# x of a Mamba2 layer brought to token order by VectorE's 32x32 blocks and DRAM instead of TensorE

## The reference, cut to what matters

```
gate, xBC, dt = split(xn @ in_proj_w.T)
x, B, C = split(silu(conv4(xBC) + conv_b))
xdt = x * dt                                    # per token and head
scores = (C @ B.T) * Lmat                       # chunk by chunk, Lmat = exp(cs_l - cs_s), lower triangle
Ydiag  = scores @ xdt
states = B.T @ (decay * xdt)                    # one per chunk, then a scan over the chunks
Yoff   = C @ prev_state * exp(cs)
y = (Ydiag + Yoff + x * D) * silu(gate), normed in each group, @ out_proj_w.T
```

## Time and profile before

| | us |
|---|---|
| median of 3 runs | 1758.66 (1757.75 to 1759.58) |
| profiled execution, its own time | 1758.21 |
| its span in the profile | 1756.4 |
| PE busy | 1742.4 |
| DVE busy | 1402.7 |
| ACT busy | 1221.6 |
| POOL busy | 1232.1 |

### The profile page before, as it was taken

One profiled execution on the slowest core, in us unless ns is written; L12 is line 12 of the kernel. 1 busy time (PEld: TensorE's weight loads), 2 busy tenths in 40 slices (PEclk: granted clock), 3 DMA queues, 4 the chain that ended last, 5 costly groups with the idle time before them and its releaser, 6 DMA issues.

```text
span 1756.4 us, 30305 instructions
## 1 busy us (share of the span) xinstructions
PE 1742.4 (99%) x10301; PEld 1459.3 (83%) x10301; DVE 1402.7 (80%) x2211; ACT 1221.6 (70%) x2456; POOL 1232.1 (70%) x877
## 2 busy tenths in 40 slices
PE   8999999999999999999999999999999999999999
PEld 6788888888888888888888888888888888888877
DVE  7978788878878788778788788878887887868941
ACT  6986677777776777777867778767877787643320
POOL 5677777777876787677776777677777787576630
PEclk9999999999999999999999999999999999999999
DMA  5442333333333343333333333333323343236522
GB/s 196 165 131 99 116 116 112 98 123 109 134 105 94 104 135 109 108 101 117 118 102 118 116 111 108 103 109 127 123 91 103 109 135 107 76 98 175 146 78 96
DMA packets 122595, 202.84 MB, mean 115 GB/s; under 512 B 23056, under 2 KB 60560, under 8 KB 122192
## 3 DMA queue, kind: packets, MB, share of 16 engines
q1 hardware_dynamic: 120720, 197.32, 34.8%
q10 hardware_dynamic: 1728, 3.65, 0.5%
HBM read 193.57 MB, written 7.34 MB: 114 GB/s over the span
## 4 chain that ended last, share of the span: by engine, by line
PE 94%; DVE 3%; issue 1%; POOL 1%; DMA 0%; ACT 0%; SPq 0%; DVEq 0%; ACTq 0%; POOLq 0%
PE bank L143 17%; PE bank L145 16%; PE bank L144 16%; PE bank L573 10%; PE bank L609 7%; PE bank L677 7%; PE bank L679 7%; PE bank L678 6%; PE bank L888 3%; PE bank L738 3%; DVE z L1246 1%; PE bank L700 0%; DVE lm L1267 0%; PE bank L720 0%; DVE acc L1337 0%
## 5 line engine op out<-in xcount | busy, mean ns | idle before, releaser
L964 ACT ACTIVATE lm<-lm,hp 128x128 f32<-128x128 f32 x1024 | 313.1, 389 | 0.8
L1246 DVE SCALAR_TENSOR_TENSOR z<-bank,cw_all,z 128x511 f32<-128x511 f32 (+2 forms) x384 | 286.9, 747 | 13.3 <-ACT z L1000 4.2
L1611 POOL TENSOR_TENSOR conv_lo<-raw_x,conv_hi 128x512 fp32r<-128x512 f32 x124 | 203.7, 1643 | 129.4 <-ACT conv_hi L901 129.3
L143 PE MATMUL bank<-xn_hi,conv_hi 128*128 128x512 f32 x640 | 261.4, 408 | 1.9 <-DVE z L1246 1.4
L1306 DVE TENSOR_TENSOR xdt<-bank,hp 128x512 f32<-128x512 f32 x128 | 88.2, 689 | 212.4 <-PE bank L738 212.4
L145 PE MATMUL bank<-xn_hi,conv_lo 128*128 128x512 f32 x640 | 250.6, 392 | 0.0
L144 PE MATMUL bank<-xn_lo,conv_hi 128*128 128x512 f32 x640 | 249.5, 390 | 0.0
L1594 POOL TENSOR_TENSOR yt<-yt,ec 128x384 f32<-128x384 f32 x128 | 146.8, 1147 | 139.3 <-DVE ec L1315 107.9
L1280 DVE SCALAR_TENSOR_TENSOR lm<-lm,gm 128x1024 f32<-128x1024 f32 x128 | 225.3, 1760 | 7.8 <-ACT lm L964 7.2
L1578 POOL TENSOR_TENSOR y_lo<-yt,y_hi 128x512 fp32r<-128x512 f32 x128 | 180.1, 1407 | 52.4 <-ACT y_hi L1035 52.4
L143 PE MATMUL bank<-xn_hi,gate_hi 128*128 128x512 f32 x512 | 212.9, 416 | 0.0
(11 more groups left out here) (152 smaller groups left out, 4051.5 us busy)
## 6 DMA issues: line engine op xcount, KB each, us to landing
lm<-cs_d SPq DMA_DIRECT2D x128, 512.0 KB, 4.5
raw_x<-w_conv_dram SPq DMA_DIRECT2D x128, 256.0 KB, 3.5
ec<-e_d SPq DMA_DIRECT2D x256, 96.0 KB, 2.7
raw_o<-w_out_dram SPq DMA_DIRECT2D x64, 256.0 KB, 3.0
raw_g<-w_gate_dram SPq DMA_DIRECT2D x61, 256.0 KB, 3.2
raw_g<-w_conv_dram SPq DMA_DIRECT2D x16, 256.0 KB, 3.2
raw_o<-w_conv_dram SPq DMA_DIRECT2D x14, 256.0 KB, 3.4
q_raw<-w1q_dram SPq DMA_DIRECT2D x10, 256.0 KB, 3.9
```

The costliest lines, as they stand in the source:

```text
L143: pe.matmul(dst, a_hi, b_hi, start=(i == 0), stop=False)
L964: e = act.activation(lm[m % LM_BUFS][:, u, :], lm[m % LM_BUFS][:, u, :], ACT.Exp, bias=hp[bd.seq][:, Q_CS, k1, u:u + 1])
L1246: dve.scalar_tensor_tensor(dst[:, d:SEQ], src[:, 0:SEQ - d], cw_all[:, bd.group, pos, 3 - d:4 - d], dst[:, d:SEQ], ALU.mult, ALU.add).then ...
L1611: pool.tensor_tensor(conv_lo[kx % 2][:, :, :], raw_x[:, kx % 2, :].rearrange("p (k j) -> p k j", k=KT), conv_hi[kx % 2][:, :, :].bitcast(F ...
```

## The change

For tiles 7 to 123 (`by_blocks`) TensorE no longer turns x. In an odd step n, VectorE transposes 32x32 blocks of `xt` of tile n+1 (even, at the start of the step) and of tile n+2 (odd, behind `ec`) into the half of `z` that is idle then. SP stores the half to DRAM (`xb_d`), waits for that, and loads it again in four DMAs of 32 partitions each, with the blocks in their place, straight into `xdt[t % 2]`. VectorE then reads `xdt` from SBUF for `xw`, and multiplies `xdt` in place. ScalarE waits for the store before it writes the half of z anew, SP waits for the diagonal of tile t-2 before it loads. Tiles 0 to 6 and 124 to 127 go as before.

```diff
+def by_blocks(t):
+    return paired(t) and t >= TILES - 1
...
+    xb_d = nc.dram_tensor("xb_d", (2, BLK, 32, NC, BLK, 32), F32).ap()
...
+            def blocks_out(t):
+                if by_blocks(t):
+                    sp.wait_ge(blk_done[t % 2], pair_blocks(t))
+                    wait(sp, xtok_in[t % 2], 16 * BLK * pair_blocks(t - 2))
+                    sp.dma_start(xb_d[t % 2].rearrange("g i c b j -> (g i) (c b j)"), z[:, t % 2, :]
+                                 ).then_inc(xb_out[t % 2], 16)
+
+            def tokens_in(t):
+                if by_blocks(t):
+                    sp.wait_ge(xb_out[t % 2], 16 * pair_blocks(t))
+                    sp.wait_ge(yd_done, t - 1)
+                    for b in range(BLK):
+                        sp.dma_start(xdt[t % 2][32 * b:32 * b + 32, :].rearrange("i (c g j) -> i c g j", c=NC, g=BLK),
+                                     xb_d[t % 2, :, :, :, b].rearrange("g i c j -> i c g j")
+                                     ).then_inc(xtok_in[t % 2], 16)
...
+                if k % 2:
+                    blocks_out(n + 1)
                 load_rows(body, k)
+                if k % 2:
+                    tokens_in(n + 1)
+                    blocks_out(n + 2)
...
+                if k % 2:
+                    tokens_in(n + 2)
                 bd, k1 = at(body, k, 1)
                 for group, pos in out_piece(bd, k1):
...
                 diag(n - 1, ps_y)
-                pe.wait_ge(xw_done, n + 1)
+                pe.wait_ge(st_done, n)
+                if not by_blocks(n):
+                    pe.wait_ge(xw_done, n + 1)
                 diag(n, ps_x)
...
                     pe.wait_ge(xw_done, n + 1)
+                    wait(pe, st_done, n)
...
-                if bd.exists():
+                if bd.exists() and not by_blocks(n + 1):
                     pe.wait_ge(xs_done, TILES * bd.n + k1 + 1)
...
                     wait(act, xs_done, m - 1)
+                    if by_blocks(m - 2):
+                        act.wait_ge(xb_out[kx % 2], 16 * pair_blocks(m - 2))
...
+                def blocks(t):
+                    if by_blocks(t):
+                        dve.wait_ge(xs_done, t + 1)
+                        dve.transpose(z[:, t % 2, :], xt[:, t % 4, :]).then_inc(blk_done[t % 2], 1)
+
+                if k % 2:
+                    blocks(n + 1)
+
                 if body.exists():
...
+                    if by_blocks(n):
+                        dve.wait_ge(xtok_in[n % 2], 16 * BLK * pair_blocks(n))
+                        if k == 0:
+                            wait_hp(dve, body)
+                        dve.wait_ge(st_mm, n)
+                        dve.tensor_tensor(by_head(xw[:, :]), by_head(xdt[n % 2][:, 0:(NC - 1) * P]),
+                                          per_token(hp[body.seq], Q_DEC, k, NC - 1), ALU.mult).then_inc(xw_done, 1)
+                        dve.wait_ge(xw_done, n + 1)
+                        dve.tensor_tensor(by_head(xdt[n % 2][:, :]), by_head(xdt[n % 2][:, :]),
+                                          per_token(hp[body.seq], Q_DT, k, NC), ALU.mult).then_inc(xdt_done, 1)
+                    else:
...
                 if pv.exists():
...
                     dve.tensor_tensor(ec[kp % 2][:, :], ps_y[:, P:NC * P], ec[kp % 2][:, :], ALU.mult
                                       ).then_inc(t0_done, 1)
+
+                if k % 2:
+                    blocks(n + 2)
```

More of the change, by code:

```diff
@@ L49 @@
 LM_BUFS = 4
+BLK = P // 32
 SH = 4
@@ L111, in paired, with blocks_before, pair_blocks @@
     return TILES // 2 <= n < TILES * (BODIES - 1) + TILES // 2
+def by_blocks(t):
+    return paired(t) and t >= TILES - 1
+def blocks_before(t):
+    return sum(1 for u in range(t) if by_blocks(u))
+def pair_blocks(t):
+    return sum(1 for u in range(t % 2, t + 1, 2) if by_blocks(u))
 def group_exists(group):
@@ L316, in build @@
         tx_done = sem("tx_done")
+        blk_done, xb_out, xtok_in = ([sem(f"{name}{i}") for i in range(2)] for name in ("blk_done", "xb_out", "xtok_in"))
         xdt_done, xw_done = sem("xdt_done"), sem("xw_done")
@@ L432, in load_rows @@
                                  .partition_broadcast(P)).then_inc(row_in[m % LM_BUFS], 16)
+            def blocks_out(t):
[12 more added lines that the diff above has]
+                                     ).then_inc(xtok_in[t % 2], 16)
             def step(body, k):
+                n = TILES * body.n + k
                 bx, kx = at(body, k, 5)
@@ L1298, in step @@
                                       None, ALU.add).then_inc(rs_done, 1)
-                if body.exists():
[L1302 to L1310, removed]
+                def blocks(t):
+                    if by_blocks(t):
+                        dve.wait_ge(xs_done, t + 1)
+                        dve.transpose(z[:, t % 2, :], xt[:, t % 4, :]).then_inc(blk_done[t % 2], 1)
@@ new lines, in step @@
+                if k % 2:
+                    blocks(n + 1)
+                if body.exists():
+                    if by_blocks(n):
[9 more added lines that the diff above has]
+                    else:
+                        dve.wait_ge(tx_done, n + 1 - blocks_before(n))
+                        if k == 0:
+                            wait_hp(dve, body)
+                        wait(dve, yd_done, n - 1)
+                        dve.tensor_tensor(by_head(xdt[n % 2][:, :]), by_head(ps_x[:, :]),
+                                          per_token(hp[body.seq], Q_DT, k, NC), ALU.mult).then_inc(xdt_done, 1)
+                        wait(dve, st_mm, n)
+                        dve.tensor_tensor(by_head(xw[:, :]), by_head(ps_x[:, 0:(NC - 1) * P]),
+                                          per_token(hp[body.seq], Q_DEC, k, NC - 1), ALU.mult).then_inc(xw_done, 1)
```

## The result

The changed kernel takes 1869.7 us (1866.4 to 1873.4, 4 runs) against 1758.7 for the kernel before in the same job: ratio 1.063 [1.061, 1.065]. It is 111 us slower. The forecast was 1738 with a range of 1710 to 1768.

What follows compares the result with a forecast made beforehand. TensorE (PE) was taken to bound the kernel, 94% of the last chain. From 1758.21 us, 51.5 came off for PE's transposes and 31.5 were added for VectorE's stalls: 1738.2, forecast 1738, range 1710 to 1768 (8 in 10).

Steps and rivals of the forecast that it cites:

- SP's queue: SP's 10 more issues per pair of steps delay raw_o by 2.2 us; costed at 0, keeping 0 to 5 us.
- Steps 1 to 3: VectorE's added work stalls PE in these steps of a body, 2.1 us in the mean over 15 bodies: 31.5 us.
- On average it all fits: VectorE's added 129 us over 117 tiles fit into its 272 us of idle time, though not everywhere.
- a slow transpose: Rival: VectorE's block transpose takes the slow form, 1.5 us, giving 1775 us in all; chance 0.19.
- late landings: Rival: the even tile's runs land 5 us or more after their last issue, giving 1765 us; chance 0.09.
- What is removed: PE does no transposes of x for 117 tiles at 0.44 us each: 51.5 us off the path.
- The block transpose: VectorE's 32x32 block transpose of 128x512 takes 0.69 us, 0.60 from start to start; upper bound 1508 ns.
- xdt and xw, +0.5 us: VectorE's two multiplications, read from SBUF beside POOL, take 0.5 us more a tile, between 0 and 1.07.
- What goes through DRAM: Store and four loads a tile: 0.56 us an issue, landing in 3.7, in time for VectorE; cost 0.
- ACT's new wait (`xb_out`): ScalarE's wait for the store before it writes z is already met (stored by 638.1, written at 640.08): cost 0.
- DMA as the bound: Rival: runs of 128 bytes are so slow that DMA binds, adding 830 us, some 2590 in all; chance 0.03.
- The profile that I announced: Signs: 0.69 us transpose, two modes in xdt and xw, PE waiting some 30 us for ec and state, nowhere else.

Runs made afterwards that it cites:

- e13: Changed kernel without block transposes and DMAs, xdt and xw multiplied out of PSUM in the old form, x left out of the computation: 1720.4 us.
- e14: As e13, with the 117 block transposes on VectorE, still no DMAs: 1741.8 us.
- e16: As e15, with the odd tile's four loads issued last in the odd step: 1747.6 us.
- e1: Changed kernel with the odd tile's four loads behind the loads of raw_o, raw_g and B's and C's weights in SP's order: 1816.4 us.
- e5: As e3, with the 117 block transposes left out too, so only the slower xw and xdt out of SBUF remain as added VectorE work: 1735.7 us.
- e15: Changed kernel with its transposes, DMAs and SP order, but xdt and xw multiplied out of PSUM in the old form: 1852.1 us.
- e3: Changed kernel without any of the DMAs; block transposes kept, xw and xdt made straight from xt in SBUF, x not turned: 1802.6 us.
- e10: As e4, with the even tile's block transpose moved behind ec in the odd step: 1746.7 us.
- e4: Changed kernel with only the even tiles (58) by blocks and DRAM, TensorE turning the odd ones: 1744.4 us.
- e7: Changed kernel with only the odd tiles (59) by blocks and DRAM, their loads issued in the following even step behind the load of lm: 1781.1 us.
- e9: As e4, with the even tile's multiplication of xdt moved to the end of its step: 1772.0 us.
- e8: Changed kernel with odd tile's loads in the following even step, both block transposes behind ec, even tile's xdt multiplication at the end of its step: 1804.0 us.

## Why the prediction was wrong

From 1758.7 to 1869.7, one term after the other, each a difference of two medians:

| step | from, to | us |
|---|---|---|
| PE's turns gone | before, e13: 1758.7 to 1720.4 | -38.3 |
| block transposes on DVE | e13, e14: to 1741.8 | +21.5 |
| the transfers, in a harmless order | e14, e16: to 1747.6 | +5.8 |
| xw and xdt out of SBUF | e16, e1: to 1816.4 | +68.8 |
| the odd tile's loads ahead of the weights | e1, after: to 1869.7 | +53.4 |

The 5.8 us are hardly more than the noise: the intervals of e14 and e16 touch. The 68.8 us hold more than two slower multiplications. From e16 to e1 the groups of xw and xdt grow by 108 us, those of the decays and scores, which nobody edited, by 27. Besides, the two change places (xdt now comes second, behind the end of xw) and PE no longer waits for xw between its two diagonals; the 15.4 us from e13 to e5 hold these too. No run tells place from duration here.

The last two rows don't add in one way only: taken first, the order costs 104.5 (e16 to e15) and the slower multiplications after it 17.6 (e15 to after). Each of the two is enough to make the kernel slower than before; which limit is reached first hides part of the other.

Two steps of the prediction failed, SP's queue ("I cost it at 0") and the stalls of "Steps 1 to 3" ("On average it all fits"). No rival had either of them: what it put on slower, 0.22, rested mostly on a slow transpose and late landings, and neither came. Point by point, by the prediction's own steps:

- **What is removed, 51.5 us.** Right in kind, mis-sized: 38.3. Each turn took 0.40 us of busy time instead of 0.44, and 9.4 us of new idle time on PE was not counted.
- **The block transpose, 0.69 us.** Right: 0.70. The slow form at 1.5 us, the rival with 0.19, does not exist here.
- **xdt and xw, +0.5 us.** Mis-sized: 2.09 for 1.24 in the groups after, so +0.85 of the +1.07 that I had as the upper bound. "On average half of that extra" was a guess; the scores' mean of 1760 between 1200 and 2314 was its only ground.
- **"On average it all fits", and stalls only in steps 1 to 3, 31.5 us.** This step failed. Transposes and slow multiplications together cost 1802.6 - 1720.4 = 82.2 us (e3 against e13). PE waits for ec in steps 1, 3 and 7, and in the same steps for y of the pair, ahead of the state's product, which the sum did not have at all. So step 7, one of those put at nothing, costs too. The two additions cost little one by one, 21.5 and (e5 against e13) 15.4 us, 36.9 in sum; together they cost more than twice that. In the loop DVE idles 245 us in e13, 169 in e14 and 94 in e3. I had booked the idle time as a store to draw from down to zero; but it lies between waits for PE, ACT and POOL, and in e3 PE was held up in three odd steps of four with more than a third of e13's idle time still unused.
- **What goes through DRAM: in time, cost 0.** Nearly right: 5.8 us in a harmless order, and DVE waits 5.0 us for it in the changed kernel. The issue of a load took 0.64 us instead of 0.56, and the landing 3.0 instead of 3.7.
- **SP's queue, "I cost it at 0 and keep 0 to 5 us".** This is the step that failed worst: 53 to 105 us, by the order in which the terms are taken. Two things were wrong in it. The delay: I counted the four issues (2.2 us) but not that SP waits, ahead of them, for the odd tile's own store to land, with `raw_o`, `raw_g`, the next `raw_x` and `lm` queued behind it; store, wait and issues take from 683.63 to 690.91 in the chain above. And the sentence "ScalarE is not where the time is set": it held in the trace of before, where ACT was busy 70% of the time, but ACT's work has an order too. Behind the late `raw_o` stand z, silu and the gate, and PE and POOL wait for the gate. (How much of the price is SP's wait and how much its issues is not separated; e1 moves both.)
- **ACT's new wait (`xb_out`) costs 0.** Right: 2.4 us of waits in the changed kernel, and with 34 us of them (e10) the time is within the noise of e4's.
- **DMA as the bound, 2590 us.** Did not happen: DMA's share rose from 0.35 to 0.51, and a load of 512 runs of 128 bytes landed in 3.0 us. The rule of the Trainium skill (VectorE: DVE Perf Modes, The three transpose paths) on plain copies that are 19 times slower than the crossbar's speaks of a large innermost stride at the destination; here it is one element within each run of 128 bytes, no such loss shows, and it was rightly left out of the sum.
- **The profile that I announced.** Of its signs the transpose, two modes in xdt and xw, and PE waiting for ec came; "nowhere else" did not.

The version that pays is e4: even tiles only. Its store and loads go out early in the odd step, and ACT's longest row of waits for weights is 14.8 us (16 times, for `raw_g`); on DVE the slower multiplications fall into the step that has no y to make. That this is why it pays is read from e4 and e7 and not tested alone. It is 0.8% faster than before.

## What to carry to other kernels

When transfers are put into a queue that works in order, count from the first wait that they bring to the last issue, and ask of each buffer behind them whether it is single (`raw_o`, `raw_g`) and who reads it next, even if that engine is idle 30% of the time. Idle time of an engine is no store to be used up: here transposes of 82 us, put on an engine with 245 us of idle time, cost 21.5 us, and the 113 us that xw and xdt take longer in e3 than in e14 cost 61. If a change as a whole loses, try it on the part of the tiles whose step has room: half of this one wins where the whole loses.

## What the runs showed of the hardware

**VectorE and GpSimd take turns when each has an operation with two inputs in SBUF.** One place of the trace after, start and duration, shows it:

```profile
605.64 1.30 POOL L1647 TENSOR_TENSOR y_lo<-yt,y_hi 128x512 fp32r<-128x512 f32 x1 [0.74 <-ACT y_hi L1082]
606.01 1.34 DVE L1362 TENSOR_TENSOR xw<-xdt,hp 128x384 f32<-128x384 f32 x1
606.90 1.61 POOL L1673 TENSOR_TENSOR sq_sum<-sq_sum,gate 128x512 f32<-128x512 f32 x1
607.38 1.68 DVE L1365 TENSOR_TENSOR xdt<-xdt,hp 128x512 f32<-128x512 f32 x1
```

xw begins while POOL is in y_lo, which ends at 606.94, and ends at 607.35, 0.41 us later, about its undisturbed 0.52. The next operation of POOL, begun at 606.90, takes 1.61 instead of about 1.3, and xdt ends 0.55 us behind it (its undisturbed duration is 0.69; POOL's records are less exact). The minimum of xw is 512 ns and that of xdt 691, their maxima 1676 and 1792: one operation and the rest of one of POOL's. The transfers are not the reason, since e3 has none and its means are 1090 and 1082 ns. ec, with one input in PSUM, keeps 0.54 to 0.56 us in all its 128 rows, and the transposes, with one input, 695 to 716 ns. The Trainium skill has this as an exclusive lock on a shared port (SBUF — State Buffer, SBUF: two separate sides): the one that starts first holds it for its whole instruction, and the other blocks. The trace agrees, and it gives the size: where POOL is busy 69% of the loop, the two inputs from SBUF cost +0.85 us on 1.24. It also offers a reason why the place of a multiplication (e9), or transposes put between (e14), change the duration of the scores, which have two inputs in SBUF too, by some 25 us in all: it shifts who meets whom. That is argued and not shown.

**TensorE's granted clock fell behind long waits of TensorE.** It was 1.0, the level of 2.4 GHz, in the whole profile before. After, it is 0.984 in the mean. One place of the trace after shows how this looks:

```profile
672.95 1.09 PE L765 MATMUL bank<-ident,sq_sum 128*128 128x128 f32 x4 [4.39 <-POOL sq_sum L1673]
...
676.40 0.63 PE L159 MATMUL bank<-xn_hi,conv_hi 128*128 128x512 f32 x1
...
678.47 0.39 PE L159 MATMUL bank<-xn_hi,conv_hi 128*128 128x512 f32 x1
```

The granted clock is 0.61 in the window from 670 to 675 us and 0.71 in the next, so parts of both went at 1.2 GHz. Behind the wait of 4.39 us a matmul of this form takes 0.63 us and the next starts 0.42 to 0.43 behind it; from 678.2 on it is 0.39 and 0.23, as in the trace before. In e15 (PE idle 102 of 1606 us) the clock is 0.983, in e16 (36 of 1506) 1.0. The sum of idle time alone does not decide it: e8, with 81 of 1561 us idle, has 0.999, and e1, with 75 of 1573, has 0.991. Some of the loss comes this way: from e16 to e15 the loop grows by 100 us, PE's idle time by 66, and its busy time by 34 with the same matmuls.
